# Result rows of a tile loaded tile by tile during the expert jobs, by thresholds worked out on the chip

## What is computed

```python
x = x + 0.5 * ffn(layernorm(x))
x = x + attn(layernorm(x))
x = x + 0.5 * ffn(layernorm(x))

# ffn: 16 experts, each token goes to 2 of them
scores = softmax(xt @ router_w + router_b) + router_bias       # groups of 4: best 2 groups, best 2 experts in them
y = sum over experts e of gate[:, e] * ((silu(xt @ w1[e] + b1[e]) * (xt @ w2[e] + b2[e])) @ w3[e] + b3[e])
z = silu(xt @ sw1 + sb1) * (xt @ sw2 + sb2) @ sw3 + sb3          # the shared expert, all tokens
return y + z
```

## Time and profile before

| | us |
|---|---|
| executions | 454.78, 451.63, 454.63 (median 454.63) |
| profiled execution, span from first to last instruction | 449.1 |
| busy PE | 394.0 (88%) |
| busy DVE | 270.9 (60%) |
| busy ACT | 174.9 (39%) |
| busy POOL | 162.9 (36%) |
| HBM read, written | 46.32 MB, 19.79 MB (147 GB/s over the span) |
| granted TensorE clock, mean | 0.992 |

### The profile page before, as it was taken

The page is one execution under the profiler, slowest core; times in us unless marked ns, Lnnn a source line. Parts: engine busy times, 40 slices in busy tenths (PEclk is TensorE's granted clock), DMA queues, the critical chain, the costliest instruction groups (busy, mean ns, idle before and its releaser), DMA issues.

```text
span 449.1 us, 8313 instructions
## 1 busy us (share of the span) xinstructions
PE 394.0 (88%) x2788; PEld 276.8 (62%) x2789; DVE 270.9 (60%) x695; ACT 174.9 (39%) x292; POOL 162.9 (36%) x230
## 2 busy tenths in 40 slices
PE   0899899999969998879979989979999879999972
PEld 0687578888647666645545555434587558888650
DVE  4579623333378954888885795666539933233357
ACT  1321246566112312166653454553441326665300
POOL 2521326665304842343432242343001054666300
PEclk9999999999999999999999999989999999999998
DMA  7999994534298569113312200010420043444278
GB/s 231 290 376 311 316 320 164 167 94 160 98 358 251 157 153 218 52 41 96 89 57 59 79 23 11 16 34 23 161 95 0 0 142 109 155 131 151 87 275 332
DMA packets 51180, 66.05 MB, mean 147 GB/s; under 512 B 8318, under 2 KB 30502, under 8 KB 51108
## 3 DMA queue, kind: packets, MB, share of 16 engines
q1 hardware_dynamic: 42780, 43.55, 30.7%
q0 software_dynamic: 6368, 19.32, 13.5%
q10 hardware_dynamic: 2000, 2.76, 2.1%
HBM read 46.32 MB, written 19.79 MB: 147 GB/s over the span
## 4 chain that ended last, share of the span: by engine, by line
PE 55%; DVE 21%; DMA 13%; SPq 4%; issue 4%; POOL 1%; ACT 1%; ACTq 0%; DVEq 0%; POOLq 0%
PE ps L1559 15%; PE ps L1566 7%; PE ps L1709 6%; PE ps L1423 5%; PE ps L1544 4%; DVE arena L1199 3%; PE ps L1685 3%; DMA turns<-in_L_ffn_sw_dram 3%; PE ps L1628 3%; DMA q_dram<-arena 3%; SPq L394 2%; PE ps L1657 2%; DMA arena<-xn_dram,arena 2%; DMA x<-_attn_hidden_states_dram 2%; PE ps L1659 2%
## 5 line engine op out<-in xcount | busy, mean ns | idle before, releaser
L1199 DVE TENSOR_REDUCE arena<-ps 128x3 f32<-128x384 f32 x128 | 68.6, 553 | 24.8 <-PE ps L1659 22.5
L1559 PE MATMUL ps<-arena,wj 128*128 128x128 f32 x608 | 74.1, 274 | 0.0
L1559 PEld LDWEIGHTS ps<-arena,wj 128*128 128x128 f32 x608 | 71.0, 192 | 1.0 <-issue 1.0
L806 ACT ACTIVATE arena<-ps 128x768 f32<-128x768 f32 x64 | 51.3, 811 | 52.0 <-PE ps L1673 51.7
L627 POOL TENSOR_SCALAR_AFFINE_SELECT arena<-arena 128x512 f32<-128x512 f32 x64 | 41.1, 642 | 78.8 <-ACT arena L806 78.4
L1096 DVE SCALAR_TENSOR_TENSOR arena<-ps,arena 128x128 f32<-128x128 f32 x38 | 13.3, 351 | 82.3 <-ACT arena L713 80.4
L1423 PE MATMUL ps<-arena,turns 128*128 128x256 f32 x256 | 57.6, 381 | 0.5 <-DMA turns<-in_L_ffn_sw_dram 0.5
L1423 PEld LDWEIGHTS ps<-arena,turns 128*128 128x128 f32 x256 | 48.1, 190 | 8.9 <-issue 2.1
L554 POOL DMA_INDIRECT arena<-xn_dram,arena x34 | 33.3, 979 | 50.7 <-DVE arena L1036 25.2
L559 POOL DMA_INDIRECT y_dram<-arena x38 | 38.5, 1012 | 34.4 <-DVE arena L1103 25.4
L1657 PE MATMUL ps<-cb 128*128 128x256 bf16 x128 | 35.4, 276 | 12.0 <-DVE arena L1199 11.4
(11 more groups left out here) (198 smaller groups left out, 601.4 us busy)
## 6 DMA issues: line engine op xcount, KB each, us to landing
arena<-y_dram SPq DMA_DIRECT2D x16, 512.0 KB, 7.7
arena<-q_dram SPq DMA_DIRECT2D x36, 128.0 KB, 2.6
xn_dram<-arena SPq DMA_DIRECT2D x16, 256.0 KB, 6.3
w<-in_L_ffn_ew_dram SPq DMA_DIRECT2D x4, 1024.0 KB, 10.5
q_dram<-arena SPq DMA_DIRECT2D x16, 192.0 KB, 2.5
x<-_attn_hidden_states_dram SPq DMA_DIRECT2D x4, 512.0 KB, 6.4
out_dram<-x SPq DMA_DIRECT2D x8, 256.0 KB, 5.4
arena<-arena SPq DMA_DIRECT2D x30, 64.0 KB
```

The costliest lines, as they stand in the source:

```text
L806: act.activation(pr[:, n % 2, pair, :], ps[:, bank:bank + 2, :].rearrange("p a b -> p (a b)")[:, 0:768], ACT.Exp).then_inc(sem("exp"), 1)
L1199: dve.tensor_reduce(m3[:, h:h + 1, :], ps[:, bank, 0:3 * P].rearrange("p (n k) -> p n k", n=3), AX_X, ALU.max).then_inc(sem("s_max"), 1)
L1559: ins = pe.matmul(o, wj[:, par, c, n * INTER:(n + 1) * INTER], xgT[:, par, c, :], start=(c == 0), stop=(c == KC - 1))
```

## The change

The stores of a layer are not waited for all together. Each tile but the last gets a threshold.

**Thresholds.** `stores_needed` (DVE, once per layer, before the first `gated`) works out from the ranks in PSUM, for each t from 0 to 6, how many jobs from the first on hold all rows of tiles 0 to t: the highest expert with a token among them, its first job, plus the jobs that its tokens of those tiles fill. Of this it makes the counts of even and odd stores, in multiples of 16, in a part of `eb` that was free. SP reads the 14 numbers into registers. With the routing above the counts of jobs are 12, 13, 14, 15, 16, 17 and 18 for tiles 0 to 6, in both layers; tile 7 waits for all 19.

**Loads.** SP waits for `s_gu` of FIRST = 6 up products, then for each of the tiles 0 to 5 for its two thresholds, and issues its load. In the first layer the load of `wq` comes next, after all up products of the jobs, then tile 6 by its thresholds, and tile 7 after all stores and `s_gu` of 8.

**Stores.** The last job's store raises `y_out{f}_0` like the other even ones, and POOL issues it only when all other even stores have landed.

**PE.** `shared_up` 6 and 7 stand ahead of `shared_down(5)`.

**DVE.** `pairs_x` 0 and 1 come right behind the last copy out of PSUM, ahead of `shared_h(6)` and of `shared_x(5)`, and the work behind them is put in another order. In the first layer DVE and ACT wait for all stores before they write what lies over the stores' sources and row lists.

```diff
+            def y_rows_due(t):
+                nc.sync.wait_ge(sem(f"y_out{f}_0"), due_at[t][0])
+                nc.sync.wait_ge(sem(f"y_out{f}_1"), due_at[t][1])
+                y_rows(t)
-            nc.sync.wait_ge(sem(f"y_out{f}_1"), outs)
-            nc.sync.wait_ge(sem(f"y_out{f}_0"), outs)
-            nc.sync.wait_ge(sem("y_end"), 16 * (f + 1))
-            y_rows(range(4))
+            nc.sync.wait_ge(sem("s_gu"), NT * f + FIRST)
+            for t in range(NT - 2):
+                y_rows_due(t)
             if f == 0:
+                nc.sync.wait_ge(sem("gu0"), all_up)
                 nc.sync.dma_start(wq, ...)
-            nc.sync.wait_ge(sem("s_gu"), NT * f + NT - 2)
-            y_rows(range(4, NT - 1))
+            y_rows_due(NT - 2)
+            nc.sync.wait_ge(sem(f"y_out{f}_1"), odd_stores)
+            nc.sync.wait_ge(sem(f"y_out{f}_0"), even_stores)
             nc.sync.wait_ge(sem("s_gu"), NT * f + NT)
-            y_rows((NT - 1,))
+            y_rows(NT - 1)
...
                 if k == LAST - 1:
-                    scatter(rowl[:, k:k + 1], 2, "y_end")
+                    pool.wait_ge(sem(f"y_out{f}_0"), others)
+                    scatter(rowl[:, k:k + 1], 2, f"y_out{f}_0")
...
+            def stores_needed():
+                seen, found, first = due[:, 0], due[:, 1], due[:, 2]
+                link(dve.tensor_scalar(duei[:], ps_rank[0:1, 1:NT, :], float(P - 1), None, ALU.add))
+                link(dve.tensor_scalar(duei[:], duei[:], P.bit_length() - 1, None, ALU.arith_shift_right))
+                link(dve.tensor_copy(seen, duei[:]))
...
+                link(dve.tensor_reduce(due_max[:], seen, AX_X, ALU.max))
...
+                dve.tensor_scalar(stores_due[:, 1, :], due_jobs[:, 0], 16.0, None, ALU.mult).then_inc(sem("due"), 1)
...
             last_rows_out(2 * rest + 4, 0)
-            shared_x(5)
+            pairs_x(0)
+            pairs_x(1)
             shared_h(6)
             if f == 1:
-                for t in range(2):
-                    pairs_x(t)
+                pairs_x(2)
+                pairs_x(3)
                 shared_h(7)
-                for t in range(2, 5):
-                    pairs_x(t)
+                pairs_x(4)
+                shared_x(5)
+                pairs_x(5)
                 shared_x(6)
-                pairs_x(5)
+                pairs_x(6)
                 shared_x(7)
-                pairs_x(6)
                 pairs_x(7)
...
-            pairs_x(0)
+            att_stats(0)
+            pairs_x(2)
             shared_h(7)
-            pairs_x(1)
-            att_stats(0)
             att_norm(0)
-            shared_x(6)
-            pairs_x(2)
-            shared_x(7)
+            shared_x(5)
             pairs_x(3)
             att_stats(1)
+            shared_x(6)
+            rows_stored()
+            att_norm(1)
+            shared_x(7)
             dve.memset(nm[:], 0.0)
             link(dve.memset(vv[:], 1.0))
+            pairs_x(4)
             rest(0, 0)
-            pairs_x(4)
-            att_norm(1)
...
             pe.wait_ge(sem(f"y_sb{f}"), 2 * rest + 4)
-            shared_down(5)
             shared_up(f, 6)
             shared_up(f, 7)
+            shared_down(5)
             pe.wait_ge(sem(f"y_sb{f}"), 2 * rest + 5)
             shared_down(6)
```

More of the change, by code:

```diff
@@ L575, in ffn_pool @@
             last = [pool.to_reg(2 * rest + k + 1) for k in range(LAST)]
+            others = pool.to_reg(16 * rest + 32)
             for k, done in enumerate(last):
@@ L749, in ffn_act @@
             silu(2 * rest + 4, 0)
+            odd_stores, even_stores = act.to_reg(16 * rest + 32), act.to_reg(16 * rest + 48)
             shared(FIRST, NT)
+            if f == 0:
+                act.wait_ge(sem("y_out0_1"), odd_stores)
+                act.wait_ge(sem("y_out0_0"), even_stores)
         def att_act():
@@ L1036, in token_list @@
                 dve.tensor_scalar(listu[:], rowu[:], TOKENS - 1, None, ALU.bitwise_and).then_inc(sem("list"), 1)
+            def stores_needed():
[3 more added lines that the diff above has]
+                link(dve.tensor_copy(seen, duei[:]))
+                link(dve.tensor_scalar(found, seen, 1.0, None, ALU.min))
+                link(dve.tensor_tensor(first, found, bc(cnt[0:1, 3:4, :], [1, NT - 1, E]), ALU.mult))
+                link(dve.scalar_tensor_tensor(out=seen, in0=seen, scalar=float(P), in1=first, op0=ALU.mult, op1=ALU.add))
+                link(dve.tensor_reduce(due_max[:], seen, AX_X, ALU.max))
+                link(dve.tensor_scalar(due_jobs[:, 0], due_max[:], 1.0 / P, 2.0, ALU.mult, ALU.max))
+                link(dve.tensor_scalar(due_jobs[:, 1], due_jobs[:, 0], 1.0, None, ALU.add))
+                link(dve.tensor_scalar(due_jobs[:, 0:2], due_jobs[:, 0:2], 1, None, ALU.arith_shift_right))
+                dve.tensor_scalar(stores_due[:, 0, :], due_jobs[:, 1], 16.0, None, ALU.mult)
+                dve.tensor_scalar(stores_due[:, 1, :], due_jobs[:, 0], 16.0, None, ALU.mult).then_inc(sem("due"), 1)
             def jobs_of_experts():
@@ L1131, in ffn_dve, with rows_stored @@
             last_rows_out(2 * rest + 4, 0)
[L1132 removed]
+            pairs_x(0)
+            pairs_x(1)
             shared_h(6)
             if f == 1:
[L1135 to L1136 removed]
+                pairs_x(2)
+                pairs_x(3)
                 shared_h(7)
[L1138 to L1139 removed]
+                pairs_x(4)
+                shared_x(5)
+                pairs_x(5)
                 shared_x(6)
[L1141 removed]
+                pairs_x(6)
                 shared_x(7)
[L1143 removed]
                 pairs_x(7)
[L1145 removed]
+            def rows_stored():
+                dve.wait_ge(sem(f"y_out{f}_1"), odd_stores)
+                dve.wait_ge(sem(f"y_out{f}_0"), even_stores)
+            return pairs_x, shared_h, shared_x, rows_stored
         chain_a = [0]
@@ L1172, in att_norm, with att_dve @@
                                   ALU.subtract, ALU.mult).then_inc(sem("a_xn"), 1)
-        def att_dve(pairs_x, shared_h, shared_x):
+        def att_dve(pairs_x, shared_h, shared_x, rows_stored):
             dve = nc.vector
```

22 lines of the change are left out of this document (16 added, 6 removed).

## The result

The changed kernel took 443.52, 440.78, 439.96 and 444.86 us, median 442.15, beside 453.94 for the kernel before in the same rounds (four executions): ratio 0.974, 95% interval 0.969 to 0.978, or 11.8 us less. The forecast was 443.1. Medians are given over all executions, while ratios leave out those that took over 1.5% longer than the fastest of the same kernel (four of the 23 of before beside e1 to e4, whose other 19 have a median of 452.7).

A forecast was written before the change was run, and what follows sets the result against it. The prediction took the end to be a stall for rows, then a DVE queue, with the same stall in the first layer. Gains of 6.35 + 5.2 = 11.5 us off 454.6 gave 443.1 us, range 440 to 449.5.

The forecast's parts named there:

- Rows early, thresholds spread: End of each layer's jobs: thresholds of 12 to 18 jobs let tile rows arrive about 3 us apart, none late.
- First layer: From the last jobs into the attention: 5.2 us less, taken between limits of 3.9 and 5.6.
- PE's 3.9: First layer, PE after the jobs: no wait left, so query products start 3.9 us earlier.
- DVE's 5.6: First layer, DVE up to the first `rest` of batch 1: that starts 5.6 us earlier.
- the first rival: First layer keeps only PE's gain or less: 6.4 to 10.2 us less in all, 444.4 to 448.2; chance 0.20.
- Second layer: End of the kernel: the last `pairs_x` ends at 440.25 instead of 446.60, a gain of 6.35 us.
- stores beside loads: Job stores running beside row loads, both layers: taken as costing nothing, 0 to 0.7 us a job for the range.
- the last store's new wait: Last job's store waiting for job 16's: that lands at 118.5, before the last is issued, so costs nothing.
- The bound of 4.05 us: Landing of a job's store standing wholly behind a 512 KB load: 4.05 us, just in time.
- signs of being wrong: `pairs_x(0)` or `rows_out` waiting for a DMA, or attention scores starting less than 4 us earlier.
- The point from which the jobs feel it, 4.3 us: Copies reusing a store's buffer: late stores decide nothing until a landing goes over 4.3 us.
- the second rival: Stores land late beside loads: up to 0.7 us a job, 7 us, 443.1 to 450.1; chance 0.17, with DMA-bound rival.

The follow-up runs named there:

- e1: The changed kernel with PE's and DVE's orders of before, keeping the thresholds and early loads: 451.57 us, ratio 0.998.
- e4: The changed kernel with the last job's store on a semaphore of its own, without waiting for the other even stores: 442.48 us, ratio 0.974.
- e3: The changed kernel with the second layer's waits, loads and orders put back to those of before: 446.40 us, ratio 0.983.
- e9: The changed kernel itself, unaltered, timed again later: 441.53 us beside 454.65 for the kernel before, ratio 0.970.
- e11: The changed kernel with the last store on its own semaphore, plus six unread 512-column matmuls in two second-layer PE waits: 441.23 us, ratio 0.970.
- e2: The changed kernel with the loads of before, SP waiting for all stores; the new PE and DVE orders stay: 456.93 us, ratio 1.010.
- e12: The kernel of e11 with a smaller filling, three and two matmuls of 256 columns: 440.94 us, ratio 0.970.
- e5: The changed kernel with thresholds as constants, without the twelve small DVE instructions and SP's register loads: 444.03 us, ratio 0.979.
- e8: The changed kernel with each load taking only the first choice's rows, half the bytes in half as many pieces: 440.45 us, one execution.

## Why the prediction held, step by step

**Rows early, thresholds spread.** Right. The first `pairs_x` starts as the last copy ends, at 117.87 and 421.94, and the first load is issued at 102.8 (103.5 forecast). The loads behind it came 1.7 to 5.0 us apart up to tile 5, not an even 3, since late stores held some of them up.

**First layer.** The sum said 5.2 in the attention's stretch; B shows 5.2, and 4.1 of it at the query products, where 3.9 was forecast. The choice between PE's 3.9 and DVE's 5.6 came out right, and the first rival, that only PE's part stays, falls. What I named as the reason, SP's and the DMAs' part of the chain, no run tested.

**A gain that the sum did not have.** e3, the first layer alone, is 7.6 us faster by its times, where B in its profile is 5.9 shorter than in that of before. And the profiled execution of before was a quick one: its span is 449.1 us, where the eleven executions beside e9 to e11 have spans of 448.9 to 454.7, median 452.9. The windows of the earlier trace rows's kind for 130 to 135 us tell why that may be. In before, with PE busy 2.48 of 5 us, the clock stayed at 1.00. Before's window:

```profile
130.00:135.00 5.00, 2.48 (x13) 1.51 (x12) 4.05 (x10) 1.07 (x2) 0.72 (x1) 1.00 1.04 388
```

In e1, with the same order on PE and the same 2.48, it fell to 0.80 and then 0.86. E1's windows:

```profile
130.00:135.00 5.00, 2.48 (x10) 1.56 (x10) 4.05 (x10) 0.22 (x1) 0.72 (x1) 0.80 0.32 106
135.00:140.00 5.00, 5.00 (x19) 3.38 (x18) 2.85 (x5) 1.21 (x3) 0.00 (x0) 0.86 0.10 11
```

B was 65.8 us there instead of 63.5. 0.5 us of that is no matter of the clock, since the turning already started 15.1 us behind the last copy instead of 14.6 (a late store had held up the copy of job 17, and PE waited 0.60 us for it). From the turning on the clock was low, and it took 1.94 us, not 1.07. E1's timeline of PE:

```profile
118.67 1.95 PE L1513 MATMUL ps<-turns,arena 128*128 128x512 f32 x4 [0.60 <-issue]
...
133.58 1.94 PE L1666 MATMUL ps<-cf,arena 128*128 128x128 f32 x8 [2.52 <-DVE arena L1219]
```

In e2 the clock fell to 0.51 behind a wait of 5.93 us that its order brings, so it says nothing on before. In after and in e3 to e12 the clock is 1.00 at this place. After's window:

```profile
130.00:135.00 5.00, 5.00 (x23) 3.60 (x22) 4.60 (x11) 0.75 (x2) 2.13 (x4) 1.00 0.77 168
```

If most executions of before lose the other 1.8 us, which its mean clock of 0.980 over those eleven executions fits (0.992 in the profiled one), then 8.9 + 1.8 = 10.7 stands beside the measured 11.8 (9.8 to 14.1) and 13.1. That is argued from the profile of another kernel; before has only the one, and a part of the gain stays without a cause.

**Second layer.** 6.35 was forecast; D is 5.3 shorter and E 1.5 longer, 3.7 in all. The mechanism was right and two terms were mis-sized. `pairs_x(7)` ended 16.4 us after the last copy instead of 15.3: `shared_x` with the `pairs_x` behind it that reads the same `x` takes 0.79 (430.59 to 431.38 in the timeline) and not 0.6, three times, and tile 7's rows came 0.46 us late. And the last store of `x`, taken as unchanged at 2.5 us, ended 4.0 us behind `pairs_x(7)`, since all stores of `x` stand in SP's queue behind tile 7's load.

**The step that failed: stores beside loads, and the last store's new wait.** "That store lands at 118.5, before the last store is issued: nothing." Job 16's store started at 115.25 and the last one, held for it, at 121.24, after a wait of 2.76 us; in the second layer the wait was 4.01. The bound of 4.05 us for a landing with the store behind a whole load was too low: 4.62 to 5.70 in the chain above, against 2.73. `rows_out` waiting for a store was one of the signs of being wrong that I had named, and it came: copies waited three times, 1.8 us in all. Two of them in DVE's timeline:

```profile
411.54 0.69 DVE L1143 COPY arena<-ps 128x512 f32<-128x512 f32 x1 [0.33 <-DMA y_dram<-arena]
...
418.48 0.69 DVE L1143 COPY arena<-ps 128x512 f32<-128x512 f32 x1 [1.09 <-DMA y_dram<-arena]
```

The point from which the jobs feel it, 4.3 us, was passed, but the last copy still stood 7.03 us behind that of job 15, as before, and PE had no wait from it. In after the second rival's cause is there, its price isn't; in e5 it cost PE 0.96 us once. (The rows that gave me 4.29 us are those of jobs 13 and 15, not 14 and 16: job 14's store started at 416.37 and job 16's copy at 420.97, 4.60 later.) From the rule of the Trainium skill, "DMA: Bandwidth & Descriptors", section "Queues, rings and completion order", I had worked out that a store loses at most its own length, 0.7 us. That working failed: the stores of the chain lost 1.9 to 3.0 us. Whether the rule itself fails isn't shown, since I had taken the turns of the two queues as equally long, and no run here measures them.

**The total.** 443.1 against 442.15 and 441.53. That it came so near is partly luck, as two errors cancel. The second layer brought 2.6 us less than forecast, which the profiles show. The first brought about 2.4 more by e3's time, which its interval alone doesn't tell from nothing. In the profiles the sum of 11.5 us is 8.9, and what the times have beyond that was not in my sum.

## What to carry to other kernels

Early data and the order that uses it are one change: either alone was worth 1 us, within the noise, or cost 4. When a transfer is moved beside others, don't price its landing from a profile in which it was alone, and look at every wait that the change adds on it, since that wait pays for the delay first. Look also at what stands behind such a wait in the same queue: here finished tiles of `x` could not leave. A stall of TensorE can cost more than its length, so a forecast from one profiled execution should look at which clock falls that execution happened to miss.

## What was not expected of the hardware

- A 256 KB scattered store that landed 2.73 us after its start alone needed up to 5.70 us with 512 KB loads beside it. With half of the pieces loaded (e8) it needed about 3.7; with half-length pieces (e6) one store still needed 5.20.
- The granted TensorE clock fell to 0.51 in the 5 us behind windows in which PE was busy 3.12 and 2.75 of 5.00, in after and not in e9, which is the same code; 2.6 us of dummy matmuls in the two waits there kept it at 1.00 at that place, and no execution of twelve had a mean below 0.989. At the lower level the first job's 16 up-product matmuls took 3.62 us, in e9, without the fall, 1.95.
- One f32 matmul of 512 columns in the program is two in the trace: three took 2.74 us, twice what I had reckoned.
